# A Mamba block and a mixture of experts on one core: convolution in plain fp32, block decays spread in another order, all engines reordered

## What is computed

```python
xn     = layernorm(layernorm(x)) * norm_w + norm_b
x_in, z = split(xn @ in_proj_w.T)                     # 256 channels each
u      = silu(conv1d(x_in, conv_w, 4 taps) + conv_b)  # full 256x256 weights per tap
delta, B, C = split(u @ x_proj_w.T)                   # 1, 16, 16
d      = softplus(delta @ dt_w.T + dt_b)
h_t    = h_{t-1} * exp(-d_t) + B_t * u_t              # 256 channels x 16 states
y_t    = h_t . C_t
x1     = x + layernorm((y * silu(z)) @ out_proj_w.T + layernorm(x))
```

## Time and profile before

| | before |
|---|---|
| median of 3 runs (range) | 1084.61 us (1083.42 to 1084.79) |
| the profiled execution: its time, its span | 1086.89 us, 1085.1 us |
| mean granted TensorE clock | 0.933 |
| PE busy | 915.2 us, 84% of the span |
| DVE, ACT, POOL busy | 68%, 68%, 62% |

### The profile page before, as it was taken

How to read it: one execution, slowest core, us unless ns; L and a number is a source line. 1 busy time by engine, 2 the same in 40 slices (tenths; PEclk the granted TensorE clock), 3 DMA queues, 4 the chain that set the end, 5 groups by cost and what they waited for, 6 DMA issues and landing times.

```text
span 1085.1 us, 26273 instructions
## 1 busy us (share of the span) xinstructions
PE 915.2 (84%) x7015; PEld 831.2 (77%) x7015; DVE 740.9 (68%) x2454; ACT 741.4 (68%) x1438; POOL 669.8 (62%) x844
## 2 busy tenths in 40 slices
PE   4888888888888888888772199999999999999873
PEld 2777767767777777777672199999999999999831
DVE  2378777877778777787665257777677777777644
ACT  3766776677776787767742177777777777877525
POOL 2454666767677766776554536666666666666648
PEclk8999998999999999999875599999999999999987
DMA  7000110111101111011108551111111111111083
GB/s 276 11 10 31 44 46 11 50 45 50 28 28 47 48 47 31 19 35 41 35 23 355 148 203 46 48 49 49 48 50 50 48 46 50 49 45 50 20 321 145
DMA packets 52192, 75.24 MB, mean 69 GB/s; under 512 B 11056, under 2 KB 32818, under 8 KB 51281
## 3 DMA queue, kind: packets, MB, share of 16 engines
q1 hardware_dynamic: 40816, 54.87, 15.8%
q0 software_dynamic: 8672, 16.93, 4.4%
q10 hardware_dynamic: 2560, 1.75, 0.6%
HBM read 47.09 MB, written 27.41 MB: 69 GB/s over the span
## 4 chain that ended last, share of the span: by engine, by line
PE 57%; issue 12%; ACT 10%; DVE 9%; POOL 9%; DMA 1%; SPq 0%; POOLq 0%; ACTq 0%; DVEq 0%
PE pA L1712 10%; PE pR L1712 10%; PE pB L1720 5%; PE pY L1720 5%; PE pY L1570 3%; PE pY L1606 3%; PE pB L1616 3%; PE pA L1436 3%; DVE y_both L1161 2%; POOL chosen_scratch L651 2%; POOL slots_scratch L606 2%; PE pA L1437 2%; ACT decS L801 2%; PE pA L1438 2%; DVE Hs L1110 2%
## 5 line engine op out<-in xcount | busy, mean ns | idle before, releaser
L651 POOL DMA_INDIRECT chosen_scratch<-yo,got_id x143 | 147.9, 1034 | 97.4 <-issue 78.9
L970 ACT ACTIVATE stage<-w_sb 128x1024 f32 x143 | 151.2, 1057 | 53.7 <-issue 37.5
L606 POOL DMA_INDIRECT slots_scratch<-xrow,send_at x128 | 140.1, 1094 | 57.1 <-issue 34.0
L1357 DVE TENSOR_TENSOR hidT<-pR,sil 128x512 f32<-128x512 f32 x143 | 98.9, 692 | 84.1 <-ACT sil L965 61.3
L1712 PE MATMUL pA<-xsT,stage 128*128 128x128 f32 x1144 | 152.2, 277 | 0.4 <-ACT xsT L954 0.4
L1712 PE MATMUL pR<-xsT,stage 128*128 128x128 f32 x1144 | 151.5, 276 | 0.0
L1712 PEld LDWEIGHTS pA<-xsT,stage 128*128 128x128 f32 x1144 | 140.1, 193 | 0.7 <-ACT xsT L954 0.7
L1712 PEld LDWEIGHTS pR<-xsT,stage 128*128 128x128 f32 x1144 | 139.4, 192 | 0.0
L641 POOL TENSOR_TENSOR ers<-eve,neg_half 128x1 f32<-128x1 f32 x143 | 81.2, 568 | 47.2 <-DVE eve L1369 45.9
L965 ACT ACTIVATE sil<-pA 128x512 f32<-128x512 f32 x143 | 85.3, 596 | 27.3 <-PE pA L1712 25.4
L548 POOL TENSOR_TENSOR R<-R,dec 128x512 f32<-128x512 f32 x48 | 60.2, 1254 | 46.9 <-ACT Rh L819 44.7
(11 more groups left out here) (201 smaller groups left out, 2306.2 us busy)
## 6 DMA issues: line engine op xcount, KB each, us to landing
got<-slots_scratch SPq DMA_DIRECT2D x143, 65.0 KB, 1.9
w_sb<-chosen_scratch SPq DMA_DIRECT2D x16, 512.0 KB, 5.2
w_sb<-in_w_dram SPq DMA_DIRECT2D x1, 4608.0 KB, 14.8
xin<-in_x_dram SPq DMA_DIRECT2D x16, 256.0 KB, 2.9
xr<-in_x_dram SPq DMA_DIRECT2D x16, 256.0 KB, 2.9
w_sb<-in_w_dram SPq DMA_DIRECT2D x1, 4096.0 KB, 14.7
x_scratch<-x SPq DMA_DIRECT2D x16, 256.0 KB, 3.2
fx<-x_scratch SPq DMA_DIRECT2D x1, 4096.0 KB, 14.9
```

Source lines behind the costliest of these rows:

```text
L606: eng.indirect_dma_start(slots_d, bass.IndirectOffsetOnAxis(ap=send_at[:, s % 2, k, t:t + 1], axis=0), xrow[:, s % 2, k, t, :], None).then ...
L651: eng.indirect_dma_start(chosen_d, bass.IndirectOffsetOnAxis(ap=got_id[:, j % NGOT:j % NGOT + 1], axis=0), yo[:, q, :], None, bounds_check ...
L970: eng.activation(stage[:, j % NSTAGE, :, :].rearrange("p k f -> p (k f)"), w13_sb[:, bass.ds(e, 1), :, :].rearrange("p o k f -> p (o k f)" ...
L1357: eng.tensor_tensor(hidT[:, p, :], pR[:, p, :], sil[:, p, :], ALU.mult).then_inc(hid_ready, 1)
```

## The change

It does four things.

1. The convolution and the gate are one plain fp32 product each, `eng.matmul(pA, taps, xn)`, in place of three. The split of the weights, `xn_hi`, `xn_lo`, `xn_high` and `xn_low` go; `xn` has two buffers now.
2. `join(8)` writes `dec16` in the order c, t, with 32 columns and not 31; `block_decay` copies the 31 columns 1 to 31 as they lie, each half with a semaphore step of its own, and a memset at the start clears column 0 of `decS` for good.
3. `load_early` loads 4 experts and `load_late` 12, in place of 7 and 9.
4. The lists in `unit` are new for POOL, ACT, DVE and PE. A semaphore per level (`r_t[h]`) takes the place of a single counter, so that levels may be in any order. SP's list is as it was.

```diff
-            def split_mm(out, hi, lo, x_hi, x_lo, start, stop):
-                eng.matmul(out, hi, x_hi, start=start, stop=False)
-                eng.matmul(out, hi, x_lo, start=False, stop=False)
-                return eng.matmul(out, lo, x_hi, start=False, stop=stop)
...
-                i = split_mm(pA[:, f, :], tap_hi[:, k, tile(f)], tap_lo[:, k, tile(f)], xn_hi[:, s % 2, w], xn_lo[:, s % 2, w], k == 0, k == TAPS - 1)
+                i = eng.matmul(pA[:, f, :], taps[:, k, tile(f)], xn[:, s % 2, w], start=k == 0, stop=k == TAPS - 1)
...
-            def split_taps():
+            def keep_taps():
                 eng.wait_ge(taps_mm, 1)
...
+                eng.tensor_copy(taps[:, :, :].rearrange("p k f -> p (k f)"), pY[:, :, :].rearrange("p a f -> p (a f)")).then_inc(taps_ready, 1)
...
-            def block_decay(s):
+            def block_decay(s, m):
                 need(eng, dec_ready, s, 4, 4)
-                need(eng, hs_ready, s, 2, 2, ago=1)
-                for m in range(2):
-                    i = eng.activation(decS[:, m, :, :].rearrange("p s (c t) -> p s c t", t=NT4),
-                                       dec16[:, m:m + 1, :].rearrange("p o (t c) -> p o c t", t=NT4).broadcast_to([P, NST, CB, NT4]), ACT.Copy)
-                i.then_inc(decs_ready, 1)
+                need(eng, h_scan, s, 2, m + 1, ago=1)
+                eng.activation(decS[:, m, :, 1:NBLK], dec16[:, m:m + 1, 1:NBLK].broadcast_to([P, NST, NBLK - 1]), ACT.Copy).then_inc(decs_ready, 1)
...
-                load_w13(0, 7)
+                load_w13(0, 4)
...
-                load_w13(7, NE)
+                load_w13(4, NE)
```

More of the change, by code:

```diff
@@ L20 @@
 W_LOADS = 11
-CONSTS = 7
+CONSTS = 6
 DEPTH = 6
@@ L80, in wait_past, with run_units @@
         eng.wait_ge(sem, value)
-def run_units(ns, unit):
-    for k in range(ns + DEPTH):
+def run_units(ns, rounds, unit):
+    for k in range(rounds):
         unit([k - j if 0 <= k - j < ns else None for j in range(DEPTH + 1)])
@@ L152, in sandwich @@
         xb = sb("xb", [P, NT4, D])
-        xn = sb("xn", [P, SEQ])
-        xn_hi = sb("xn_hi", [P, 2, SEQ + 4], f32r)
-        xn_lo = sb("xn_lo", [P, 2, SEQ + 4], f32r)
+        xn = sb("xn", [P, 2, SEQ + 4])
         RT = sb("RT", [P, 3, 2, 2, P])
@@ L495, in _ @@
         def _(eng):
-            for t, v in ((neg_half[:, :], -0.5), (half[:, :], 0.5), (G[:, AT[8], :, :], 0.0), (xn_hi[:, :, 0:TAPS - 1].bitcast(fp32), 0.0), (xn_lo[:, :, 0:TAPS - 1].bitcast(fp32), 0.0), (dec16[:, :, 0:1], 0.0), (Hs[:, :, 0:1], 0.0)):
+            for t, v in ((neg_half[:, :], -0.5), (half[:, :], 0.5), (G[:, AT[8], :, :], 0.0), (xn[:, :, 0:TAPS - 1], 0.0), (decS[:, :, :, 0:1], 0.0), (Hs[:, :, 0:1], 0.0)):
                 eng.memset(t, v).then_inc(const_ready, 1)
@@ L616, in unit @@
                 join(q[3], 1)
+                send(q[6], 3)
                 carry(q[3], 2)
@@ L622, in unit @@
                 join(q[3], 8)
-                send(q[6], 3)
+                address(q[5])
                 rstd_3(q[4])
@@ L1304, in unit @@
                 gated(q[4])
+                positions(q[5])
+                mask(q[3], 2)
+                diagonal(q[3])
+                odd(q[3])
                 mask(q[3], 4)
-                mask(q[3], 2)
-                odd(q[3])
-                positions(q[5])
-                stats_1(q[0])
-                diagonal(q[3])
+                aggr_1(q[0])
                 attend(q[4])
                 stats_3(q[4])
+                var_1(q[0])
                 aggr_3(q[4])
                 var_3(q[4])
-                aggr_1(q[0])
-                var_1(q[0])
                 shift_3(q[4])
-                scan(q[3], 0)
-            run_units(NS, unit)
+                margin(q[5])
+            run_units(NS, NS + DEPTH, unit)
             eng.wait_ge(pos_step, 3 * NS)
@@ L1470, in project_gate @@
                 w = slice(TAPS - 1, TAPS - 1 + SEQ)
-                split_mm(pA[:, 1 - f, :], gate_hi[:, tile(f)], gate_lo[:, tile(f)], xn_hi[:, s % 2, w], xn_lo[:, s % 2, w], True, True).then_inc(in_mm, 1)
+                eng.matmul(pA[:, 1 - f, :], gate_w[:, tile(f)], xn[:, s % 2, w], start=True, stop=True).then_inc(in_mm, 1)
             def project_state(s):
@@ L1646, in unit @@
             def unit(q):
-                odd_turn(q[4])
-                gram(q[4], 2)
                 r_turn(q[4], 2)
                 gram(q[4], 4)
+                gram(q[4], 2)
+                rank(q[6])
                 project_gate(q[3], 1)
-                rank(q[6])
-                conv(q[3], 1, 0)
+                odd_turn(q[4])
+                project_out(q[5])
+                gram(q[4], 8)
+                r_turn(q[4], 4)
                 level(q[4], 2)
-                project_out(q[5])
                 r_turn(q[4], 8)
-                r_turn(q[4], 4)
-                gram(q[4], 8)
+                level(q[4], 4)
                 r16_turn(q[4], 0)
@@ L1661, in unit @@
                 level(q[4], 8)
-                level(q[4], 4)
+                conv(q[3], 1, 0)
                 states(q[4], 0)
+                states(q[4], 1)
                 x_turn(q[2])
-                states(q[4], 1)
                 h_turn(q[4], 0)
@@ L1672, in unit @@
                     conv(q[3], 1, k)
+                conv(q[2], 0, 0)
                 project_state(q[3])
-                conv(q[2], 0, 0)
+                conv(q[2], 0, 1)
+                xf_turn(q[5])
+                next_b(q[3])
                 delta_turn(q[3])
-                next_b(q[3])
-                for k in range(1, 3):
-                    conv(q[2], 0, k)
-                xf_turn(q[5])
+                conv(q[2], 0, 2)
                 route(q[5])
                 bc_turn(q[3], 0)
-                conv(q[2], 0, 3)
                 diag_turn(q[3])
                 bc_turn(q[3], 1)
+                conv(q[2], 0, 3)
                 project_gate(q[2], 0)
-            run_units(NS, unit)
+            run_units(NS, NS + DEPTH, unit)
             eng.wait_ge(lg_read, NS)
```

128 lines of the change are left out of this document (52 added, 76 removed).

## The result

The changed kernel takes 1050.51 us (median of 4 runs, 1048.31 to 1052.16). Beside it the kernel before took 1084.7. The ratio is 0.9667, with a 95% interval of 0.9633 to 0.9702: 3.3% faster. The forecast was 1042 us and 1024 to 1066. The time falls inside the range, in my likeliest case (1026 to 1056), 8.5 us above its middle.

What follows compares the result with a forecast made beforehand. Stage one was taken as bound by a ring of waits between engines, not PE's work alone. Rounds -38.7, start -5 and end +1.5 gave -42 us off the median of 1084.6: 1042 us, range 1024 to 1066.

Steps and rivals of the forecast that it cites:

- my likeliest case: Whole kernel: a time of 1026 to 1056 us, chance 0.56.
- The round: One repeat of stage one's steady loop, 15 in all: from 34.18 down to 31.6 us, -38.7 us in sum.
- a ring of waits: Stage one: engines waiting on each other in a circle, not PE's work alone, set a round's 34.2 us.
- Logits' idle, -1.1: First half of a round, DVE: its 1.14 us wait for `route` goes as `xf_turn` and `route` come earlier.
- The meeting, -1.4: First half: `send 3` beside `choose` and `gated` keeps `carry 2` off DVE; `chosen_b` -1.0, `gated` -0.4 us.
- Second half, +0.2 - 1.1: From `gated` to `from_state`'s end: later path to r16 +0.2, block decays with `yh_copy 4` ahead -1.1; 16.5 to about 15.5 us.
- Products, +0.2: PE's plain fp32 products, 0.86 us apiece against 0.77 for a group of three: +0.2 us a round.
- Overlooked waits, +0.5: Whole round: an allowance of 0.5 us on the walked 31.1 for waits missed, giving 31.6.
- The start: Up to the first `y_first` (57.2 before): DVE's earlier beginning -3, no `xn_hi` and `xn_lo` -2; sum -5 (-2 to -8).
- The end: Behind the last `y_first`: the late load grows to 12 experts and a send may wait longer, +1.5 us (0 to +5).
- The meeting fails: Rival: POOL's sends end late or the spread stays at 1.08; a round of 32.6 to 33.4, 1057 to 1069 us, chance 0.22.
- PE becomes the bound at half clock: Rival: longer fp32 products at a granted clock of 0.88 make a round 35.2 us, 1096 us in all; chance 0.07.

Runs made afterwards that it cites:

- e_send: Changed kernel with POOL's send 3 put back behind join 8, as before the change; ratio to the kernel before 0.9647.
- c_placed: Changed kernel with the second half of DVE's positions step (`placed` and its sum) put behind attend; ratio to the kernel before 0.9510.
- a1_fp32: Kernel before with plain fp32 convolution and gate products and the first load split 4 to 12, old order and old decays; ratio to the kernel before 0.9993.
- r_route: Changed kernel with `xf_turn` in PE's list put back behind the third convolution product; ratio to the kernel before 0.9736.
- j_copy: Changed kernel with `yh_copy 4` in ACT's list put back behind both spreads of the block decays; ratio to the kernel before 0.9689.
- s_start: Changed kernel with the 4 MB load of the second expert weights put behind the loads of sequences 2 and 3; ratio to the kernel before 0.9637.
- k_one: `g_both` with the first of send 3's two transfers moved ahead of `carry 1` on POOL; ratio to the kernel before 1.0043.
- g_both: Changed kernel with both the edit of `c_placed` and the edit of `s_start`; ratio to the kernel before 0.9452.
- a12_parts: Kernel before with the plain fp32 products and the new form of the block decays together, in the old order; ratio to the kernel before 0.9930.
- a2_spread: Kernel before with the new form of the block decays alone, in the old place and order; ratio to the kernel before 0.9963.

## Why the prediction was right, and where it was wrong

**The round**, forecast 31.6, is 31.62. The mechanism, a ring of waits that the new order shortens, is right; that the number is right to 0.02 is luck, for some of its terms are off and cancel.
- *Logits' idle, -1.1.* It went (-1.14), and with it waits of 0.36 and 0.20 for `xs` and `next_b`: 11.0 us from `from_state` to `logits` are now 9.3, where my walk had 9.8. Undoing the place of `xf_turn` brings back 0.47. I put all of the 1.1 down to it; the other half is not shown, and the half clock and the rest of the list are the candidates.
- *The meeting, -1.4.* It took place and gave DVE 1.4. As a term of the sum it is wrong: its counter-item, `placed` +1.78, was missing. I had looked at who escapes `carry 2` and not at who runs into it instead. `e_send` shows the net of the two as nothing. Also, `with_diagonal`, which I had at 0, went from 1.86 to 2.11.
- *Second half, +0.2 - 1.1.* Measured from 16.5 to 17.1; in `c_placed`, where `placed` is out of the way, it is 15.6. So the sum of the walk, 15.5, was right to 0.1. Its split is not borne out: undone alone, the place of `yh_copy 4` is worth 0.16, and the form 0.26 (I took 0.65 us for the spread; it is 0.61). What they are worth together stays open.
- *Products, +0.2.* A product takes 0.86 us, as forecast. With the clock back at 1.00, PE is busy 29.04 us in a round, less than the 29.3 before, although its products are longer. In the old order `a1_fp32` gained 0.14 where I had a loss.
- *Overlooked waits, +0.5.* The allowance covered what `placed` took beyond the other gains. It was an allowance and no insight.
- Of the order's 2.12 us, `r_route` and `j_copy` explain 0.6. Where the other 1.5 us lie stays open: PE's list around `project_out`, DVE's masks and the rest of ACT's list were not tried one by one.

**The start**, forecast -5 (-2 to -8), is +2.9. This is the step that failed: it is 7.9 us of the error, of which the end gave 2.0 back (the span fell by 36.1 us where I had 42; the medians fell by 2 us less than the span, which is the rest of the 8.5). Its terms at the head, -3 and -2, came true together (first product 6.2 us earlier). What failed is the step from there to the first `y_first`: I summed what became shorter at the head and walked no list for sequence 0. The runs split the 7.9. In `a1_fp32`, with the old lists, the first product is 7.1 us earlier, `project_state` (29.43, before 32.31) 2.9 and the first `y_first` 1.0: so 4 of the 5 us that I forecast do not arrive even in the old order; on what they are lost stays open. The other 3.9, from -1.0 to +2.9, come with the new lists. In the first units, where half of each list is empty, an order made for the steady round puts sequence 0 behind a load; `s_start` takes the load away and has -1.8.

**The end**, +1.5, is -0.5. The late load grew by 3.0 us, where I had worked out 4.9. The send beside it still waits, 1.80 us (2.14 before):

```profile
563.66 0.96 POOL L592 DMA_INDIRECT slots_scratch<-xrow,send_at  x1 [1.80 <-issue]
585.52 8.09 SPq L464 DMA_DIRECT2D got<-slots_scratch  x8
```

Stage two starts to load at 585.52, 51.1 us behind the last `y_first` where it was 53.6, and takes 463.5 us from there where it took 461.5, though I had it untouched; the 2.0 us are not explained.

**The rivals.** "The meeting fails" had the right neighbourhood and the wrong consequence: its failing costs nothing here. "PE becomes the bound at half clock" had the sign reversed: PE idles less and keeps its clock.

The Trainium skill, page "SBUF — State Buffer", section "Who interferes with whom", says that whoever issues first holds the shared ports for the whole instruction, and that copies and casts can need them too. The rows of `k_one` agree in how long VectorE is held: 3.84 us for `with_diagonal`, 1.62 for a cast of 8 elements. They do not agree in who goes first: by the starts in the trace, rough as they are on POOL, both VectorE operations began ahead (by 0.24 us of `carry 1`, by 0.29 of `carry 2`) and ended behind. It also says that a VectorE operation with both inputs in SBUF contends with GpSimd's reads. `placed` is one, and its 2.06 us agree; I had applied the rule to `chosen_b`, `gated` and `with_diagonal`, and not to `placed`.

## What to carry to other kernels

When an order takes one VectorE operation out of a GpSimd operation's way, look for the one that takes its place: the exclusion moves, and only what is off the path may carry it. Walk the first and the last units of a pipeline with their own loads, not with the steady round's. And an order that is tuned to a tenth of a microsecond is a fit: one transfer moved past two operations turned a kernel 5.5% faster than before into one 0.4% slower.

## What the runs showed that I had not expected

- A VectorE operation can be passed by two GpSimd operations in a row (3.84 us for 1.21 of work, L1122 in `k_one`), or squeeze in between them (2.11 in the changed kernel, with `join 1` at 2.02 where `k_one` has 1.05). In the first case it started 0.24 us ahead of `carry 1`, in the second 0.47 behind it.
- An 8-element cast, 0.30 us in the changed kernel, takes 1.62 in `k_one`, where it ends with GpSimd's `carry 2`.
- The granted clock of a steady round is 1.00 in the changed kernel, `g_both` and even `a1_fp32`, 0.95 to 0.96 in `a12_parts`, and 0.90 or 0.95, from round to round, in `a2_spread` and `k_one`. What holds it in the one and not in the other stays open.
